# Four groups of convolution taps loaded, rounded and split one by one, and a new order of the first eight tiles, in a grouped convolution with a quantised dense layer

## What is computed

```python
def _L0_cond_ref(x, c, weight, c_weight, bias):      # x (64, 64, 1024), 4 groups of channels, 9 taps
    out = lax.conv_general_dilated(x, weight, window_strides=(1,), padding=[(4, 4)],
        dimension_numbers=('NCH', 'OIH', 'NCH'), feature_group_count=4)
    ctx = jnp.einsum('nd,od->no', c, c_weight)
    return out + ctx[:, :, None] + bias[None, :, None]

def _L0_ffn_ref(x, kernel, bias):                    # kernel (1024, 1024)
    xq = _fake_quant(x, bits=8, axis=-1)             # abs-max over the row, round, scale back
    kq = _fake_quant(kernel, bits=8, axis=0)
    y = jnp.einsum('bsd,df->bsf', xq, kq)
    y = y + _fake_quant(bias, bits=16, axis=-1)[None, None, :]
    return _fake_quant(y, bits=8, axis=-1)

x = x + _L0_ffn_ref(_L0_cond_ref(x, ...), L0_ffn_kernel, L0_ffn_bias)
```

## Time and profile before

| | |
|---|---|
| median of 3 runs | 250.9 us (250.19 to 253.15) |
| profiled execution, device time | 250.28 us |
| its span, first to last instruction | 248.2 us |
| PE busy | 233.9 us, 94% of the span |
| DVE, ACT, POOL busy | 206.7, 183.9, 191.1 us (83%, 74%, 77%) |
| chain that ended last | 87% PE, 6% DVE, 2% transfers |

### The profile page before, as it was taken

One profiled execution on the slowest core, in us unless ns is written; L12 is line 12 of the kernel. 1 busy time (PEld: TensorE's weight loads), 2 busy tenths in 40 slices (PEclk: granted clock), 3 DMA queues, 4 the chain that ended last, 5 costly groups with the idle time before them and its releaser, 6 DMA issues.

```text
span 248.2 us, 3979 instructions
## 1 busy us (share of the span) xinstructions
PE 233.9 (94%) x1306; PEld 148.8 (60%) x1306; DVE 206.7 (83%) x421; ACT 183.9 (74%) x182; POOL 191.1 (77%) x135
## 2 busy tenths in 40 slices
PE   7799999999999999999999999999999999999920
PEld 4478577756666666566656666665666666656400
DVE  3799897867888898778997897899798979877894
ACT  4589788866777877577598769867897975966652
POOL 4674270339999999889849986995999599989980
PEclk9999999999999999999999999999999999999995
DMA  6996600193227789996889999999989999968938
GB/s 222 399 414 251 254 1 3 17 343 111 86 24 228 171 203 342 200 364 172 170 202 282 193 282 253 248 216 356 209 224 325 241 367 204 284 116 203 417 140 333
DMA packets 16388, 56.29 MB, mean 227 GB/s; under 512 B 2288, under 2 KB 2416, under 8 KB 16368
## 3 DMA queue, kind: packets, MB, share of 16 engines
q1 hardware_dynamic: 11808, 42.08, 46.8%
q0 software_dynamic: 3744, 13.63, 30.9%
q10 hardware_dynamic: 816, 0.33, 0.5%
HBM read 39.26 MB, written 16.78 MB: 226 GB/s over the span
## 4 chain that ended last, share of the span: by engine, by line
PE 87%; DVE 6%; DMA 2%; issue 1%; POOL 1%; ACT 0%; SPq 0%; DVEq 0%
PE dense_ps L691 42%; PE conv_ps L635 35%; PE turn_ps L671 6%; PE small_ps L661 2%; DMA xwin<-x_windows 2%; PE dense_ps L711 1%; DVE a_int L924 1%; DVE y_max L950 1%; DVE small_ps L895 1%; POOL x_lo L324 1%; PE conv_ps L691 1%; DVE y L890 1%; DVE last_max L975 0%; DVE k_max L846 0%; ACT x_hi L441 0%
## 5 line engine op out<-in xcount | busy, mean ns | idle before, releaser
L691 PE MATMUL dense_ps<-kq,a_t 128*128 128x512 bf16 x496 | 115.5, 379 | 0.0
L324 POOL TENSOR_TENSOR x_lo<-xwin,x_hi 128x1032 fp32r<-128x1032 f32 x32 | 81.8, 2571 | 30.1 <-ACT x_hi L441 25.6
L332 POOL TENSOR_TENSOR y<-y,bq 128x512 f32<-128x512 f32 x60 | 81.4, 1448 | 10.9 <-DVE y L881 10.9
L691 PEld LDWEIGHTS dense_ps<-kq,a_t 128*128 128x128 bf16 x496 | 47.2, 100 | 49.0 <-issue 2.0
L895 DVE TENSOR_REDUCE small_ps<-conv_ps 128x8 f32<-128x1024 f32 x32 | 39.3, 1227 | 17.2 <-PE conv_ps L635 17.2
L501 ACT ACTIVATE y_int<-y,y_inv 128x1024 int16<-128x1024 f32 x31 | 35.6, 1148 | 18.0 <-DVE y_inv L936 17.9
L881 DVE SCALAR_TENSOR_TENSOR y<-dense_ps,row_scale,k_scale_b 128x512 f32<-128x512 f32 x58 | 43.1, 745 | 6.0 <-PE dense_ps L691 6.0
L486 ACT CAST a_t<-turn_ps 128x1024 bf16<-128x1024 int16 x32 | 32.3, 1010 | 20.6 <-PE turn_ps L671 20.5
L635 PE MATMUL conv_ps<-x_hi,w_hi 128*128 128x512 f32 x128 | 40.1, 435 | 1.4 <-ACT x_hi L441 1.4
L924 DVE TENSOR_TENSOR a_int<-conv_ps,inv 128x1024 int16<-128x1024 f32 x32 | 39.2, 1224 | 0.0
L441 ACT CAST x_hi<-xwin 128x1032 fp32r<-128x1032 f32 x32 | 33.7, 1053 | 6.4 <-DMA xwin<-x_windows 6.4
(11 more groups left out here) (67 smaller groups left out, 154.6 us busy)
## 6 DMA issues: line engine op xcount, KB each, us to landing
xwin<-x_windows SPq DMA_DIRECT2D x32, 516.0 KB, 6.6
out<-y SPq DMA_DIRECT2D x30, 512.0 KB, 4.2
y<-x_rows POOLq DMA_DIRECT2D x26, 512.0 KB, 7.4
k_raw<-ffn_kernel SPq DMA_DIRECT2D x8, 512.0 KB, 7.8
x_sb<-x_rows SPq DMA_DIRECT2D x6, 512.0 KB, 7.3
w_raw<-taps SPq DMA_DIRECT2D x2, 256.0 KB, 3.3
b_row<-ffn_bias SPq DMA_DIRECT2D x1, 512.0 KB, 10.0
out<-x_sb SPq DMA_DIRECT2D x1, 512.0 KB, 3.1
```

Of the source, the lines that this page charges most:

```text
L324: pool.tensor_tensor(x_lo[:, at].rearrange("p n b -> p (n b)"), xwin[:, t % XWIN, :], x_hi[:, at].bitcast(F32).rearrange("p n b -> p (n b) ...
L332: pool.tensor_tensor(y[:, t % YRING, half(h)], y[:, t % YRING, half(h)], bq[:, half(h)], ALU.add).then_inc(s["biased1" if h else "biased_e ...
L691: mm = pe.matmul(dense_bank(t, h), a_t[:, t % LEVELS, q].rearrange("b j o -> b (j o)"), kq[:, q, half(h)], start=(q == 0), stop=(q == Q - 1))
```

## The change

- The taps lie in memory by group: four loads of 128 KB (1 KB a partition) in place of two of 256 KB. Each group g is rounded (`round_w(g)`, 256 columns in place of 512) and split (`split_w(g)`) by itself, and the convolution of tile t < 4 waits for the remainder of its own group only.
- SP: group 0, window 0, group 1, ...; groups 2 and 3 come after window 2 and block 3. Blocks 6 and 7 move ahead of windows 6 and 7, and the bias behind window 7.
- ACT: `round_w(2)` and `round_w(3)` stand between `round_x(2)` and `seed(2)`. `scales_out()` moves: it stood behind `take_levels(3)`, it now stands behind `take_levels(4)` and `k_take(6)`. `seed(8)` moves behind `round_x(8)`.
- DVE: `k_scales(0)` moves behind `column_max(0)`, `k_scales(1)` behind `levels(1)`; several maxima of the dense kernel move behind a step of the tiles.
- POOL: each `split_w(g)` just ahead of `split` of a tile near it; `split(8)` moves ahead of the first two `add_bias`.
- PE: two more warm-up matmuls in front of the first convolution (`WARM_X` 4) and two behind it (`WARM_C0`), and the steps of tiles 2 to 7 in another order.

```diff
-WARM, WARM_G0, WARM_X = 3, 1, 2
+WARM, WARM_G0, WARM_X, WARM_C0 = 3, 1, 4, 2
...
+        w_raw = sb("w_raw", [P, GROUPS, 2, Q, CG], F32)
+        w_hi = sb("w_hi", [P, GROUPS, 2, Q, CG], F32R)
+        w_lo = sb("w_lo", [P, GROUPS, 2, Q, CG], F32R)
...
+            def load_w(g):
+                sp.dma_start(w_raw[:, g].rearrange("p c q o -> p (c q o)"), wt[:, taps_of(g)]
+                             ).then_inc(w_in[g], 16)
...
             load_w(0)
+            load_xwin(0)
             load_w(1)
-            load_xwin(0)
+            load_x(0)
             load_k(0)
+            load_x(1)
             load_k(1)
-            load_x(0)
             load_xwin(1)
             load_k(2)
             load_xwin(2)
-            load_x(1)
+            load_w(2)
             load_k(3)
+            load_w(3)
             load_xwin(3)
+            load_xwin(4)
             load_k(4)
-            load_xwin(4)
             load_k(5)
+            load_xwin(5)
+            load_k(6)
+            load_xwin(6)
+            load_k(7)
+            load_xwin(7)
             load_bias()
-            load_xwin(5)
-            load_xwin(6)
-            load_xwin(7)
-            load_k(6)
-            load_k(7)
             load_scales()
             load_xwin(8)
...
             split_w(0)
+            split(0)
             split_w(1)
-            split(0)
             split(1)
+            split_w(2)
             split(2)
+            split_w(3)
             split(3)
             split(4)
             split(5)
             split(6)
             split(7)
+            split(8)
+            add_bias(0, 0)
             add_bias(0, 1)
-            add_bias(0, 0)
-            split(8)
             add_bias(1, 0)
             add_bias(2, 0)
             split(9)
...
             round_w(0)
+            round_x(0)
             round_w(1)
-            round_x(0)
             seed(1)
             round_x(1)
             k_round(0)
             k_round(1)
             round_x(2)
+            round_w(2)
+            round_w(3)
             seed(2)
-            k_take(0)
             round_x(3)
             take_levels(0)
+            k_take(0)
+            seed(3)
             k_take(1)
-            seed(3)
             k_take(2)
-            round_x(4)
             k_take(3)
             k_take(4)
+            round_x(4)
+            seed(4)
             take_levels(1)
-            seed(4)
-            take_levels(2)
+            round_x(5)
             k_round(4)
-            k_round(5)
-            round_x(5)
-            k_take(5)
             round_x(6)
             seed(5)
+            take_levels(2)
+            k_take(5)
+            k_round(5)
             take_levels(3)
+            seed(6)
+            take_levels(4)
+            k_take(6)
             scales_out()
             k_round(6)
-            k_take(6)
+            round_x(7)
             k_round(7)
-            seed(6)
-            take_levels(4)
+            seed(7)
             k_take(7)
-            round_x(7)
+            bias_levels()
             k_take(8)
-            seed(7)
             take_levels(5)
-            bias_levels()
+            take_levels(6)
+            round_x(8)
             seed(8)
-            round_x(8)
-            take_levels(6)
             round_x(9)
...
+                    if t < GROUPS and w is w_lo:
+                        pe.wait_ge(s["w_lo_made"], t + 1)
...
             conv(2)
+            turn_levels(1)
             k_turn(2)
-            turn_levels(1)
+            conv_start(3)
             k_turn(3)
-            conv_start(3)
             k_turn(4)
             spread_max(2)
             conv_rest(3)
             dense(0, 0)
+            conv_start(4)
+            spread_max(3)
             turn_levels(2)
-            conv_start(4)
+            conv_rest(4)
+            k_turn(5)
             dense(1, 0)
-            k_turn(5)
-            spread_max(3)
-            conv_rest(4)
+            conv_start(5)
+            spread_max(4)
+            turn_levels(3)
             dense(2, 0)
-            turn_levels(3)
+            conv_rest(5)
+            turn_levels(4)
             k_turn(6)
-            spread_max(4)
-            conv_start(5)
-            conv_rest(5)
             dense(3, 0)
-            k_turn(7)
-            turn_levels(4)
             spread_max(5)
             conv(6)
+            k_turn(7)
+            turn_levels(5)
+            dense(4, 0)
             k_turn(8)
-            dense(4, 0)
-            turn_levels(5)
             spread_max(6)
             conv(7)
             dense(0, 1)
+            spread_max(7)
+            turn_levels(6)
             dense(5, 0)
-            turn_levels(6)
-            spread_max(7)
             dense(1, 1)
...
             k_maximum(0)
             k_maximum(1)
+            column_max(0)
             k_scales(0)
-            column_max(0)
             k_maximum(2)
             levels(0)
             column_max(1)
             k_maximum(3)
+            levels(1)
             k_scales(1)
-            levels(1)
             k_round(2)
             k_round(3)
             column_max(2)
             k_maximum(4)
             levels(2)
+            column_max(3)
             k_maximum(5)
+            k_scales(2)
             scale_half(0, 0)
-            k_scales(2)
-            column_max(3)
-            k_maximum(6)
-            scale_half(1, 0)
             levels(3)
             column_max(4)
+            scale_half(1, 0)
+            k_maximum(6)
+            levels(4)
             k_maximum(7)
+            scale_half(2, 0)
             k_scales(3)
-            scale_half(2, 0)
-            levels(4)
             column_max(5)
...
```

More of the change, by code:

```diff
@@ L62, in build @@
         warm = sb("warm", [P, 2], F32)
-        w_raw = sb("w_raw", [P, 2, Q, GROUPS, CG], F32)
-        w_hi = sb("w_hi", [P, 2, GROUPS, Q, CG], F32R)
-        w_lo = sb("w_lo", [P, 2, GROUPS, Q, CG], F32R)
+        w_raw = sb("w_raw", [P, GROUPS, 2, Q, CG], F32)
+        w_hi = sb("w_hi", [P, GROUPS, 2, Q, CG], F32R)
+        w_lo = sb("w_lo", [P, GROUPS, 2, Q, CG], F32R)
         cond_all = sb("cond_all", [C_DIM, N + C + GROUPS], F32)
@@ L120, in build @@
             "y_max_made", "y_scale_made", "y_inv_made", "y_rounded", "y_dequantised", "added", "finished", "last_max", "last_rounded", "last_made")}
-        w_in = [sem(f"w_in{i}") for i in range(2)]
+        w_in = [sem(f"w_in{i}") for i in range(GROUPS)]
         xwin_in = [sem(f"xwin_in{i}") for i in range(XWIN)]
@@ L142, in half, with taps_of @@
             return slice(h * HALF, (h + 1) * HALF)
+        def taps_of(g):
+            return slice(g * 2 * Q * CG, (g + 1) * 2 * Q * CG)
         def second_step(t):
@@ L201, in _ @@
         def _(sp):
-            def load_w(ch):
-                sp.dma_start(w_raw[:, ch].rearrange("p q g o -> p (q g o)"), wt[ch]
-                             ).then_inc(w_in[ch], 16)
+            def load_w(g):
+                sp.dma_start(w_raw[:, g].rearrange("p c q o -> p (c q o)"), wt[:, taps_of(g)]
+                             ).then_inc(w_in[g], 16)
             def load_k(fb):
@@ L311, in _, with split_w @@
                                ).then_inc(s["ident_made"], 1)
[L313 to L316, removed]
+            def split_w(g):
+                pool.wait_ge(s["w_hi_made"], g + 1)
+                pool.tensor_tensor(w_lo[:, g], w_raw[:, g], w_hi[:, g].bitcast(F32), ALU.subtract
                                    ).then_inc(s["w_lo_made"], 1)
@@ L431, in _, with round_w @@
             act.copy(ident_b[:], ident[:]).then_inc(s["ident_b_made"], 1)
-            def round_w(ch):
-                act.wait_ge(w_in[ch], 16)
-                act.copy(w_hi[:, ch], w_raw[:, ch].rearrange("p q g o -> p g q o")
+            def round_w(g):
+                act.wait_ge(w_in[g], 16)
+                act.copy(w_hi[:, g], w_raw[:, g]
                          ).then_inc(s["w_hi_made"], 1)
@@ L630, in terms @@
                         wait(pe, "lo_made", t + 1)
-                    if t == 0 and w is w_lo:
-                        pe.wait_ge(s["w_lo_made"], 2)
+                    if t < GROUPS and w is w_lo:
+                        pe.wait_ge(s["w_lo_made"], t + 1)
                     for ch in range(2):
@@ L636, in terms @@
                                 conv_ps[:, at, hs, :].rearrange("p (n b) -> p n b", n=NH),
-                                w[:, ch, g].rearrange("p q o -> p (q o)"),
+                                w[:, g, ch].rearrange("p q o -> p (q o)"),
                                 x[:, x_at, hs * NH:(hs + 1) * NH, ch:ch + BLOCKS],
@@ L651, in conv_rest @@
                 terms(t, ((x_hi, w_lo), (x_lo, w_hi))).then_inc(s["conv_made"], 1)
+                for i in range(WARM_C0 if t == 0 else 0):
+                    warm_up(dense_ps[:, i % 2, :])
             def conv(t):
@@ L1016, in _ @@
             column_max(6)
+            scale_half(4, 0)
             levels(6)
-            scale_half(4, 0)
             column_max(7)
```

(4 more changed lines are left out.)

## The result

| | before | after |
|---|---|---|
| median of 20 runs each | 250.6 us | 252.33 us |
| ratio, 95% interval | | 1.0059 [1.0038, 1.0081] |
| profiled execution: span | 248.2 us | 250.2 us |

The direction and both mechanisms were as forecast, the size was not: 1.5 us by the ratio and 1.9 by the profiled executions (250.28 to 252.22), where the sum had 4.2.

The account below looks back on a forecast made before the run. PE was taken to bound the kernel, gapless from tile 2 on. 250.28 us plus 1.4 at tile 2's start plus 2.8 around tile 8 gave 254.5 us; own range 253.2 to 255.9, wider range 251.6 to 256.0.

Parts of the forecast that it names:

- both mechanisms: DVE's scale held by POOL before tile 2, costing 1.4 us, and scales sent late before tile 8, costing 2.8 us.
- What bounds the kernel: PE, gapless from tile 2's convolution at 17.56 us, so any delay to PE behind that is added to the end.
- (a): Front: with fewer taps ahead, window 0 lands near 5.7 us and window 1 near 10.27 us.
- (b): Front on PE: added warm-ups cost nothing; tile 0 ends at 10.57 us, against 11.54 before, winning 1.0 us.
- (c) the hold: DVE: `k_scales(0)` waits 1.8 us for POOL's split of tile 1, to 13.85 us; `k_inv` is made at 14.06.
- (d) S: Start of tile 2's convolution, 17.56 us before: ACT's list up to `seed(2)` puts it at 18.95, 1.4 us later.
- (e) the late scales: ACT sends the scales 4.0 us later than before; PE waits 2.8 us around `dense(1, 1)` and tile 8.
- My lower bound: Least wait around tile 8: 1.8 us, if ACT issues the scales' transfer while `k_take(6)` still runs.
- The same set: 38.83: PE from tile 2 to tile 8: same matmuls in another order, 38.83 us of gapless work as before.
- the rivals built on a short trip: Scales return in time, deciding at 5.7 us: with DVE held 251.7 us, chance 0.05; front's gain kept 249.9, 0.10.
- (f) POOL: POOL's `split(8)`, four `add_bias`, then `split(9)` end 8.7 us after tile 8 starts; PE needs 9.05: hidden by 0.35.
- Rival 4: Slower: the clock falls in the new gaps of PE; chance 0.06.

Follow-up runs that it names:

- e4: Kernel after, order untouched, with the `tensor_scalar` of `k_scales(0)` over 128x2 written as two of 128x1: 250.48 us, ratio 0.9986.
- e1: Kernel after with `k_scales(0)` put back ahead of `column_max(0)`: 250.26 us, ratio 0.9972.
- e5: Kernel before with only `k_scales(0)` moved behind `column_max(0)`: 251.97 us, ratio 1.0054.
- e7: Kernel after with `scales_out()` one instruction later, behind `k_round(6)`: span 249.6 us in a single execution, time not compared.
- e6: Kernel before with only `scales_out()` moved behind `take_levels(4)`: 254.69 us, ratio 1.0152.
- e2: Kernel after with `scales_out()` ahead of `take_levels(4)` and `k_scales(3)` ahead of `scale_half(2, 0)`: 251.55 us, ratio 1.0032.
- e10: Kernel after with `seed(8)` ahead of `round_x(8)`: 252.13 us, ratio 1.0026.
- e3: Kernel after with the edits of e1, e2 and e10: 250.39 us, ratio 0.9951.
- e8: e3 with `seed(2)` ahead of `round_w(3)` as well: 250.1 us, ratio 0.9973.
- e9: e8 with POOL's first two `add_bias` ahead of `split(8)`: 250.02 us, ratio 0.9943.
- e11: e6 with `take_levels(6)` ahead of `seed(8)` and `round_x(8)`: 254.16 us, ratio 1.0109.

## Why the prediction was right or wrong, point by point

- **What bounds the kernel** held: every difference at tile 10 is found again at the end; from the start of tile 10 to the end of the span every one takes 177.95 to 177.98 us.
- **(a), (b) the windows.** Window 0 at 5.31 (I had 5.7), window 1 at 10.24 (10.27). The context came earlier too, so the warm-ups started at 5.51, not 6.50, and tile 0 ended at 10.14, not 10.57. That was luck: the six matmuls that turn the context took 0.83 us in this execution and 1.38 in e4, which has the same front and started tile 0 at 7.51. Tile 2 hangs on window 1, so it cost e4 nothing. The two added warm-ups hid as forecast.
- **(c) the hold** is shown: by e1, e4 and e5 together, and by every held instance ending 0.02 to 0.03 us after POOL. It was 2.0 us and not 1.8, since tile 0 ended earlier: the earlier front paid for a longer hold. The Trainium skill's rule in "SBUF — State Buffer", section "Who interferes with whom", agrees with these traces. e4 adds the limit: one column is not held.
- **(d) S** was 18.73, not 18.95. PE's wait was shared by `seed(2)` (18.68) and the spread (18.64). Term right: 1.17 us against 1.4.
- **(e) the late scales** is the step that failed in size: the mechanism was right, the term was 2.8 us and 0.83 was measured. Of the 2.0 us between them, 1.5 is one sentence: "it and `k_take(6)` need 0.91 each: S + 23.6". The transfer went out at S + 22.13. I let ACT issue it when its turn in the list came; ACT's queue issued it as soon as nothing ahead was waiting for another engine, 0.05 us after the end of `k_turn(6)` (the turn started at 40.20 and took 0.61), while `take_levels(4)` still ran and `k_take(6)` had not begun. e7 shows that for two instructions ahead, and e6 that it is the wait and not a fixed distance. My lower bound named the case with 1.0 us less, and it was not enough. The other 0.5 us are the trip, 8.36 and not 8.52, window 8, 6.77 and not 7.07, and the steps behind it. At tile 8 either repair removes the wait, earlier scales (e2) or an earlier seed (e10); that it is the scales shows at tile 10, where e10 gives back 0.2 us and e2 1.0.
- **"The same set: 38.83"** was nearly right: with no wait the new order reaches tile 8 at S + 38.48 to 38.63 (e2, e3, e8, e9). The wait itself thus cost 1.0 us, and the new order gave 0.2 back.
- The trip of 2 KB was 8.36 us. The 2.0 us of the Trainium skill's page "DMA: Bandwidth & Descriptors", section "Anatomy of one DMA — SWDGE (gpsimd) path", are given there for transfers that GpSimd issues. This one goes out from ACT's queue, and the measurement decides: the rivals built on a short trip fell.
- **(f) POOL** "hidden by 0.35 us": in the kernel after just hidden (`split(9)` ends at 67.23, PE starts at 67.30), and the first thing to bind once `seed(8)` stands ahead of `round_x(8)` (e3, e10). With the scales in time and the seed behind (e2) it stays hidden.
- **Rival 4** did not happen in the kernel after, whose waits behind tile 2 are 0.4 us and less. In e6 the clock did fall, for an estimated 1.7 us. My argument against it, that the clock stood for 2.4 us after the last matmul, was too weak: there it fell behind a wait of 2.06 us, whatever the cause.

## What to carry to other kernels

Take the time of a transfer from when the last wait ahead of it in its engine's list is met, as in all the traces here, not from when the work ahead of it is done; and a small transfer to memory and back deserves its own row in the budget. Before moving a short DVE instruction, look at what POOL does at the new place: here 0.2 us became 2.2. When an order list is worked out anew, check each long-latency step against its old issue time, and ask for every wait that is removed which queue comes next: here the seed put ahead of a rounding cleared tile 8 and made POOL, which waits for that rounding, late by 0.8 us. Try repairs in pairs too: e1 with e2, which the estimate above favours, was not run.

## What the runs showed of the hardware that I had not expected

- A `tensor_scalar` over 128x2 in SBUF that comes while POOL runs a `tensor_tensor` ends 0.02 to 0.03 us after it (0.34 to 2.31 us in place of 0.17); over 128x1 it does not wait (0.20 us for two, e4).
- ACT issues a transfer ahead of two of its own instructions that stand before it in the list (e7).
- 2 KB written to memory from 128 partitions took 7.9 to 8.5 us to be reported in all fourteen profiled executions, with next to nothing else in flight (DMA share 0.05 or less in before, after, e3 and e6).
- The granted clock fell to the lower level in e6, 0.9 us after the end of a wait of PE of 2.06 us, and stood there from 58.4 to 61.8 us under full work; it did not fall in e11 with waits of 1.65 and 1.07 us. That the wait is the cause is not shown.
